# Layer 3 of a four-layer kernel on one core: lanes outside the heads in the skewed returns, a return per half of the heads, rolls built on 128 partitions, halved key and value blocks, and a new instruction plan

## The reference, cut to what matters

```python
Qf = jnp.fft.rfft(Q, axis=2); Kf = jnp.fft.rfft(K, axis=2)     # K, V padded from 154 to 1024 rows
corr = jnp.fft.irfft(Qf * jnp.conj(Kf), n=Lloc, axis=2)
corr_mean = corr.mean(axis=-1)                                  # (batch, head, shift)
w, idx = jax.lax.top_k(corr_mean, top_k)                        # top_k = 6
w = jax.nn.softmax(w, axis=-1)
rolled = jnp.take_along_axis(V[:, :, None, :, :], shifted[..., None], axis=3)
out = jnp.einsum('bhk,bhkld->bhld', w, rolled)
```

## Time and profile before

| | |
|---|---|
| runs | 1690.18, 1690.42, 1696.91 us, median 1690.42 us |
| span of the profiled execution | 1689.5 us, 0.9 us below the median |
| busy | PE 1316.3 us (78%), DVE 1113.8 (66%), ACT 816.4 (48%), POOL 690.3 (41%) |
| mean granted clock of TensorE | 0.865 |

### The profile page before, as it was taken

One profiled execution on the slowest core, in us unless ns is written; L12 is line 12 of the kernel. 1 busy time (PEld: TensorE's weight loads), 2 busy tenths in 40 slices (PEclk: granted clock), 3 DMA queues, 4 the chain that ended last, 5 costly groups with the idle time before them and its releaser, 6 DMA issues.

```text
span 1689.5 us, 18810 instructions
## 1 busy us (share of the span) xinstructions
PE 1316.3 (78%) x5858; PEld 660.2 (39%) x5858; DVE 1113.8 (66%) x2929; ACT 816.4 (48%) x2055; POOL 690.3 (41%) x705
## 2 busy tenths in 40 slices
PE   5789886756788687586576778768979977886998
PEld 2345443332254334333224433433533533532444
DVE  5542417689986867998989898787732451436355
ACT  2345442757657677565674577567426220310110
POOL 2000000388888888828888688875000100000000
PEclk8789997977889797779587689789989988898999
DMA  5000000376556767717656666654010211021000
GB/s 221 22 1 1 10 5 3 81 180 183 151 158 164 197 155 218 185 36 187 173 165 217 175 176 182 166 153 127 7 16 1 82 39 31 1 51 45 1 13 25
DMA packets 59381, 169.07 MB, mean 100 GB/s; under 512 B 15632, under 2 KB 20304, under 8 KB 58640
## 3 DMA queue, kind: packets, MB, share of 16 engines
q0 software_dynamic: 40960, 134.25, 29.6%
q1 hardware_dynamic: 18320, 33.61, 6.2%
HBM read 163.00 MB, written 4.82 MB: 99 GB/s over the span
## 4 chain that ended last, share of the span: by engine, by line
PE 34%; POOL 31%; issue 12%; DVE 12%; DMA 6%; ACT 4%; SPq 1%; POOLq 0%; DVEq 0%; ACTq 0%
POOL bufR L1841 26%; PE psum L1174 6%; POOL half_sum L1855 4%; PE psum L1040 3%; PE psum L1118 2%; DVE bufB L1531 2%; DMA bufR<-in_table,rowid 2%; PE psum L1097 2%; PE psum L844 2%; PE psum L1052 2%; PE psum L975 2%; PE psum L967 1%; PE psum L811 1%; PE psum L896 1%; PE psum L893 1%
## 5 line engine op out<-in xcount | busy, mean ns | idle before, releaser
L1841 POOL DMA_INDIRECT bufR<-in_table,rowid x512 | 549.1, 1072 | 247.2 <-issue 124.5
L1199 ACT ACTIVATE bufR<-bufR 128x256 f32<-128x256 f32 x512 | 205.6, 405 | 79.8 <-DVE bufR L1404 79.4
L1404 DVE TENSOR_TENSOR bufR<-bufR 128x1024 f32<-128x1024 f32 x128 | 163.1, 1275 | 63.7 <-DMA bufR<-in_table,rowid 63.5
L1040 PE MATMUL psum<-xtf,wf 128*128 128x512 f32 x320 | 158.5, 641 | 29.3 <-DVE x_sb L1467 13.3
L844 PE MATMUL psum<-bufB 32*128 32x308 f32 x768 | 99.8, 597 | 102.5 <-DVE bufB L1531 80.2
L1531 DVE TENSOR_REDUCE bufB<-psum 128x8 f32<-128x1232 f32 x96 | 137.8, 1436 | 50.5 <-PE psum L844 50.2
L1868 POOL TENSOR_TENSOR x_sb<-x_sb,wattn 128x256 f32<-128x256 f32 x16 | 11.0, 728 | 295.4 <-DMA wattn<-in_attn 165.0
L1052 PE MATMUL psum<-wf,bufR 128*128 128x256 f32 x320 | 91.1, 437 | 35.7 <-DVE bufR L1679 33.4
L1208 ACT ACTIVATE bufR<-bufR,ew 128x256 f32<-128x256 f32 x128 | 64.1, 503 | 113.0 <-DVE ew L1412 113.0
L1861 POOL TENSOR_TENSOR x_sb<-x_sb,wattn 128x256 f32<-128x256 f32 x32 | 25.4, 823 | 227.9 <-DMA wattn<-in_attn 169.9
L1467 DVE TENSOR_TENSOR x_sb<-x_sb,psum 128x256 f32<-128x256 f32 x128 | 50.1, 415 | 97.9 <-PE psum L975 62.9
(11 more groups left out here) (236 smaller groups left out, 2534.8 us busy)
## 6 DMA issues: line engine op xcount, KB each, us to landing
bufR<-in_table,rowid POOLq DMA_INDIRECT x512, 4.3
wf<-in_ffn SPq DMA_DIRECT2D x2, 2304.0 KB, 15.3
bufR<-in_ffn SPq DMA_DIRECT2D x1, 2696.5 KB, 17.2
wattn<-in_attn SPq DMA_DIRECT2D x4, 641.0 KB, 6.0
wf<-in_rope SPq DMA_DIRECT2D x4, 512.0 KB, 6.2
bufB<-in_ffn SPq DMA_DIRECT2D x1, 2048.0 KB, 8.4
scr_corr<-bufR SPq DMA_DIRECT2D x16, 128.0 KB, 2.4
bufR<-scr_corr SPq DMA_DIRECT2D x4, 512.0 KB
```

What stands on the lines that cost most here:

```text
L1040: ins = mm(bank(6 + r), gu[:, kt, r, :], xtf[:, kt, :], start=kt == 0, stop=kt == KT - 1)
L1199: own.mark(act(row, row, ACT.Identity, accum_out=dots[:, g % 4, j:j + 1]))
L1404: tt(rows, rows, cast(xg[c % 2][:, i, :].unsqueeze(1), [P, GRP, D]), ALU.mult).then_inc(f1_mu, 1)
L1841: eng.indirect_dma_start(ring[:, s * GRP + j, :], None, io["table"], bass.IndirectOffsetOnAxis(ap=rowid[c % 2][:, at + j:at + j + 1], axis ...
```

## The change

1. The skewed returns have the lanes as their first dimension (16 lanes, 8 heads for the correlation; 16 lanes, 4 heads for the rolls). The partition order inside a half becomes (lane, head), so the stores, the value fetch and the masks are rearranged to match. The fetch of the rolls is now four DMAs of 64 partitions instead of two of 128.
2. Each half g has its own return `cr b g`, behind its own stores, and its own semaphores; `o3 b g` waits only for the rolls of its half.
3. The rolls are built on 128 partitions, 8 per head with 128 positions each. `tw b` on DVE makes the weights, `tw b` on PE copies a head's places and weights to its 8 partitions by one matmul, and `tq b` on DVE makes six `tensor_scalar` of 128x128 and one `reduce_sum`. The copy of the sums out of PSUM is gone.
4. A key or value block is 64 columns for a step instead of 128 (half of the old columns were zeros that no matmul read), 128x640 an instruction; all of them lie side by side, so `ks3 1` and `vs3 1` wait for no other reader.
5. The numbers of the planner are new (`vr` counts 14.0 us instead of 1.6, PREFER holds other offsets, by prefixes of an item), so all engines' lists are in another order, in all layers.

```diff
-            a = add("ACT", ("co", b, g), 1.1, p, attn_free, b and ("SP", ("rr", b - 1)))
-            stored = add("SP", ("cw", b, g), 0.4, a, land=2.5)
-        turned = add("SP", ("cr", b), 0.2, (stored, 0.0), values, land=3.5)
+            a = add("ACT", ("co", b, g), 1.1, p, attn_free, b and ("SP", ("rr", b - 1, 1)))
+            stored = add("SP", ("cw", b, g), 3.6, a, land=2.5)
+            turned = add("SP", ("cr", b, g), 0.6, (stored, 0.0), values, land=4.5)
         p = add("PE", ("tp", b), 1.6, turned, a)
-        t = add("DVE", ("tp", b), 4.0, p)
+        t = add("DVE", ("tp", b), 2.8, p)
         a = add("ACT", ("tp", b), 0.3, t)
-        for n in range(TOPC):
-            t = add("DVE", ("tq", b, n), 1.5 if n else 3.2, a, t)
-        stored = add("SP", ("rw", b), 0.2, t, land=2.2)
-        return add("SP", ("rr", b), 0.2, (stored, 0.0), land=4.5)
+        t = add("DVE", ("tw", b), 1.4, a, t)
+        p = add("PE", ("tw", b), 0.3, t)
+        t = add("DVE", ("tq", b), 2.6, p)
+        stored = add("SP", ("rw", b), 0.8, t, land=2.2)
+        return [add("SP", ("rr", b, g), 1.2, (stored, 0.0), land=4.5) for g in range(2)]
 
     def rolled(b, rolls, values):
         for g in range(2):
-            p = add("PE", ("o3", b, g), 8.7, rolls, values)
+            p = add("PE", ("o3", b, g), 8.7, rolls[g], values)
...
-    keys = [add("DVE", ("ks3", b), 3.0, keys0, attn_free if b else ring_free) for b in range(B)]
-    values = [add("DVE", ("vs3", 0), 3.0, values_in)]
+    keys = [add("DVE", ("ks3", b), 1.5, keys0, ring_free) for b in range(B)]
+    values = [add("DVE", ("vs3", b), 1.5, values_in) for b in range(B)]
     rolls = correlate(0, keys[0], queries_in[:2], values[0])
-    values.append(add("DVE", ("vs3", 1), 3.0, values_in, ("PE", ("co", 0, 1))))
...
-        kind = item[:2] if item[0] in BY_LAYER else item[:1]
-        rank[engine, item] += PREFER.get(engine, {}).get(kind, 0.0)
+        offsets = PREFER.get(engine, {})
+        rank[engine, item] += sum(offsets.get(item[:n], 0.0) for n in range(1, len(item) + 1))
...
+        spread = late[0:H, LC["spread"]]
         c1 = [R(1040 * g, 1040) for g in range(2)]
         c2 = [R(2080 + T * g, T) for g in range(2)]
-        cor, rollw, rollt = R(0, T), R(T, T), [R(2 * T, T), R(3 * T, T)]
-        topw, topj, topjf, rsum3, topm = (R(5440 + 8 * z, 8) for z in range(5))
+        hits, rollw = R(0, TOPC * P).rearrange("p (n t) -> p n t", n=TOPC), R(TOPC * P, P)
+        topjf, topw, topj, rsum3, topm = (R(5440 + 8 * z, 8) for z in range(5))
+        topjw, onto = R(5440, 16), R(5480, 16)
         topj = topj.bitcast(U32)
 
         def kst(b, g):
-            at = bufB[:, g * U * P:(g + 1) * U * P] if b else C(g * U * P, U * P)
-            return at.rearrange("p (u n) -> p u n", u=U)
+            return C((2 * b + g) * U * HALF, U * HALF).rearrange("p (u n) -> p u n", u=U)
 
         def vst(b, g):
-            return C((0 if b else 2 * U * P) + g * U * P, U * P).rearrange("p (u n) -> p u n", u=U)
+            return C((4 + 2 * b + g) * U * HALF, U * HALF).rearrange("p (u n) -> p u n", u=U)
 
         def roll(b, g):
             return qx[b][:, g, :]
...
+            def spread_top(b):
+                eng.wait_ge(tp_w, b + 1)
+                mm(psum[:, 2, 0:16], spread, topjw[0:H, :], start=True, stop=True).then_inc(tp_s, 1)
+
             def out3(b, g):
-                eng.wait_ge(tp_rd, 32 * (b + 1))
+                eng.wait_ge(tp_rd[g], 32 * (b + 1))
                 eng.wait_ge(k3_vb, b + 1)
...
             def keys3(b):
                 ring_left(eng)
-                if b:
-                    attention_left(eng)
-                else:
+                if b == 0:
...
-                shape = [P, U, 8, 16]
-                mask = cast(mask8.unsqueeze(1).unsqueeze(3), shape)
+                shape = [P, U, 16, 4]
+                mask = cast(maskk.unsqueeze(1).unsqueeze(1), shape)
                 for g in range(2):
                     src = k3t[:, g, b * SP_:(b + 1) * SP_].rearrange("p (u s) -> p u s", u=U)
-                    ins = tt(kst(b, g).rearrange("p u (h s) -> p u h s", h=8), cast(src.unsqueeze(2), shape), mask, ALU.mult)
+                    ins = tt(kst(b, g).rearrange("p u (s h) -> p u s h", h=4), cast(src.unsqueeze(3), shape), mask, ALU.mult)
                 ins.then_inc(k3_kb, 1)
...
             def values3(b):
                 ring_left(eng)
-                if b:
-                    eng.wait_ge(co_c, 2)
                 eng.wait_ge(k3_rd, 16 * 32)
-                shape = [P, U, 8, 16]
-                mask = cast(mask8.unsqueeze(1).unsqueeze(3), shape)
+                shape = [P, U, 4, 16]
+                mask = cast(maskv.unsqueeze(1).unsqueeze(3), shape)
                 for g in range(2):
-                    ins = tt(vst(b, g).rearrange("p u (h d) -> p u h d", h=8), cast(v3s[:, 2 * b + g].unsqueeze(2), shape), mask, ALU.mult)
+                    ins = tt(vst(b, g).rearrange("p u (h d) -> p u h d", h=4), cast(v3s[:, 2 * b + g].unsqueeze(2), shape), mask, ALU.mult)
                 ins.then_inc(k3_vb, 1)
             def top(b):
                 r = slice(0, H)
                 eng.wait_ge(co_m, b + 1)
-                own.link(eng.tensor_copy(cor[r, :], psum[r, 0:2, :].rearrange("p a n -> p (a n)")))
-                own.link(eng.max(topm[r, :], cor[r, :]))
-                own.mark(eng.max_index(topj[r, :], topm[r, :], cor[r, :]))
+                cor = psum[r, 0:2, :].rearrange("p a n -> p (a n)")
+                own.link(eng.max(topm[r, :], cor))
+                own.mark(eng.max_index(topj[r, :], topm[r, :], cor))
                 tt(topw[r, :], topm[r, :], cast(topm[r, 0:1], [H, 8]), ALU.subtract).then_inc(tp_n, 1)
 
-            def rolls(b, n):
+            def weights3(b):
                 r = slice(0, H)
-                if n == 0:
-                    weights3(b, r)
-                out = rollt[n % 2] if n else rollw
-                own.link(ts(out[r, :], iota[r, :], topjf[r, n:n + 1], topw[r, n:n + 1], ALU.is_equal, ALU.mult))
-                if n:
-                    own.link(tt(rollw[r, :], rollw[r, :], out[r, :], ALU.add))
-                if n == TOPC - 1:
-                    eng.sem_inc(tp_r, 1)
-
-            def weights3(b, r):
                 eng.wait_ge(tp_n, b + 1)
                 own.wait()
                 own.link(eng.tensor_copy(topjf[r, :], topj[r, :]))
...
-                own.link(ts(topw[r, :], topw[r, :], rsum3[r, 1:2], None, ALU.mult))
+                ts(topw[r, :], topw[r, :], rsum3[r, 1:2], None, ALU.mult).then_inc(tp_w, 1)
+
+            def rolls(b):
+                eng.wait_ge(tp_s, b + 1)
+                own.link(eng.tensor_copy(onto, psum[:, 2, 0:16]))
+                for n in range(TOPC):
+                    own.mark(ts(hits[:, n, :], iota, onto[:, n:n + 1], onto[:, 8 + n:9 + n], ALU.is_equal, ALU.mult))
+                own.wait()
+                eng.reduce_sum(rollw, hits.rearrange("p n t -> p t n"), AX.X).then_inc(tp_r, 1)
 
...
                         for h in range(8):
-                            eng.dma_start(v3s[h * 16:(h + 1) * 16, 2 * b + g], src[h]).then_inc(k3_rd, 16)
+                            r, lane = h // 4 * HALF, h % 4
+                            eng.dma_start(v3s[r + lane:r + HALF:4, 2 * b + g], src[h]).then_inc(k3_rd, 16)
...
             def store_corr(b, g):
                 a = 2 * b + g
                 eng.wait_ge(co_s, 2 * b + g + 1)
+                rows = scr1[a].rearrange("(s r h) n -> r s h n", r=2, h=4)
                 for r in range(2):
                     for N in range(2):
-                        eng.dma_start(scr1[a, half(r), N * 512:(N + 1) * 512], c1[g][half(N), r * 512:(r + 1) * 512])\
-                            .then_inc(co_wr, 16)
-                    eng.dma_start(scr1[a, half(r), T:T + 16], c1[g][half(0), r * 512:r * 512 + 16]).then_inc(co_wr, 16)
-
-            def turn_corr(b):
+                        eng.dma_start(rows[r, :, :, N * 512:(N + 1) * 512], c1[g][half(N), r * 512:(r + 1) * 512])\
+                            .then_inc(co_wr[g], 16)
+                    eng.dma_start(rows[r, :, :, T:T + 16], c1[g][half(0), r * 512:r * 512 + 16]).then_inc(co_wr[g], 16)
+
+            def turn_corr(b, g):
                 attention_left(eng)
-                eng.wait_ge(co_wr, 16 * 12 * (b + 1))
-                for g in range(2):
-                    src = bass.AP(scr1.tensor, (2 * b + g) * P * (T + 16), [[16 * (T + 16), 8], [T + 17, 16], [1, T]])
-                    eng.dma_start(c2[g], src).then_inc(co_rd, 16)
+                eng.wait_ge(co_wr[g], 16 * 6 * (b + 1))
+                src = bass.AP(scr1.tensor, (2 * b + g) * P * (T + 16), [[8 * (T + 16) + 1, 16], [T + 16, 8], [1, T]])
+                eng.dma_start(c2[g], src).then_inc(co_rd, 16)
 
             def store_rolls(b):
                 eng.wait_ge(tp_r, b + 1)
                 for z in range(2):
```

(13 more changed lines are left out.)

53 lines of the change are left out of this document (28 added, 25 removed).

## The result

The changed kernel takes 1636.98 us (median of 4 runs, 1635.19 to 1639.68), the kernel before 1693.66 on the same chip (1690.18 to 1699.21): ratio 0.9673, 95% interval 0.9646 to 0.970. The forecast was 1636 us.

What follows compares the result with a forecast made beforehand. No single engine was taken as the bound, but POOL's fetches and PE's layers 2 and 3, with PE waits to close. Terms -11-22.5-20-3+2 = -54.5 us from 1689.5 gave span 1635, time 1636 us; range 1616 to 1660, 8 in 10.

Steps and rivals of the forecast that it cites:

- The bound: Whole kernel: no single engine bounds it; gains must come where POOL's chain of fetches or PE's chain stands still.
- A: Layer 3's value blocks: the addition to x_sb moves ahead of them, shrinking PE's 10.36 us wait; -11 us, bounds -12.5 to -5.
- The 32 DMAs are as long as before: Step at the value blocks: SP's issue of the value fetch stays at 15.12 us, values there 21 us after `V3`.
- B: Layer 3, round 0: PE's idle and cold matmuls at `tp 0` and `o3 0 0` vanish; -22.5 us, bounds -24 to -16.
- C: Layer 3, round 1: PE's waits at `tp 1`, the `u3` and `o3 1` and cold matmuls shrink; -20 us, bounds -23.5 to -12.
- D: Table fetches: DVE's earlier `ix1` for chunk 2 shortens POOL's longest wait, 22.35 us, to near 19; -3 us.
- The rival that ended slower: Table fetches: POOL misses turns waiting for DVE's additions, 4.61 us each, 12 more cancel the gain; 14 give 1700 us; chance 0.04.
- E: First 60 us: keys of layer 0's second batch row now stand ahead of the first head pair; +2 us, bounds 0 to +5.
- Lanes outside: Layer 3's returns: 16 lanes as first dimension bring the DMA share near 1 instead of 0.51; returns land before PE comes.

Runs made afterwards that it cites:

- e7: Changed kernel with the value DMAs writing 16 adjoining partitions instead of every fourth, output not the reference's; `V3` to the end 405.2 us.
- e4: Changed kernel with values stored in another order in DRAM, fetched by 8 DMAs of 64 partitions instead of 32 of 16; 1625.66 us, ratio 0.9646.
- e10: Kernel before with only the planner's new numbers, old operations, on the chip of e9 and e11; 1675.14 us, ratio 0.9894.
- e2: Changed kernel with the rolls built as before, in one piece on 16 partitions; 1658.41 us, ratio 0.9804.
- e11: Changed kernel, unchanged, profiled again on the chip of e9 and e10; 1634.57 us, ratio 0.9667.
- e9: Kernel before, unchanged, profiled on the chip of e10 and e11; first to last fetch 846.5 us.
- e5: Kernel before with only the planner's new numbers, old operations, on another chip than e10; 1692.39 us, ratio 0.9967.
- e6: Changed kernel with the planner's old numbers, all new operations kept; 1666.26 us, ratio 0.9802.
- e8: Version of e4 with the keys of layer 0's second batch row put back behind the first head pair's score work; 1644.47 us, ratio 0.9646.
- e1: Changed kernel with each skewed return cut in two DMAs of eight lanes; 1638.31 us, ratio 0.969.

## Why the prediction was right, by its steps

- **The bound.** No single engine, but PE's waits in layer 3: shown. The rounds gave 49.4 of the 58.3 us, at the same matmuls.
- **A, value blocks: -11 forecast, -4.8 measured** (last fetch to `co 0`; -7.6 in one pair of profiles and -1.9 in the other). From the end of `V3` on it is only -3.1 (105.3 and 105.4 before, 102.5 and 102.1 changed). The step that failed is "The 32 DMAs are as long as before". Issue took 20.6 us instead of 15.1, since every DMA now writes each fourth partition (e7), and started 1.7 us later behind `V3`; the values were there 28.2 us after `V3`'s end instead of 21, and PE waited 3.9 to 6.6 us instead of my 1.5. With an issue of 15.2 us (e7) or 5.4 (e4), `V3` to `co 0` is 95.4 and 93.9 us, -10 and -11.4 against before. The new plan with the old operations reaches 95.2 (e10). So the place and the mechanism were right, the gain is the plan's, and one price was wrong: the new order of lanes takes 7 of the 10 us back.
- **B, round 0: -22.5 forecast, -27.8 measured.** Each step stood as I had put it, counted from `co 0 1`: `tp 0` 13.2 us after its end (forecast 13.5), `tw 0` 23.8 (24.7), `o3 0 0` 38.1 (39.9). The term was mis-sized by 5.3 us, in three parts (means of the two pairs). Slow matmuls gave 8.0 us, and I had counted 5.6, in `tp` and `o3` alone; in the profiles shown above they gave 9.1, most of the rest in the last `y2` (3.44 to 1.97 us) and the logits behind it (3.54 to 1.92). Idle time gave 19.9 us where I had 18.3. And the 1.4 us that I had taken off for `tw 0` and waits inside don't show in these sums.
- **C, round 1: -20 forecast, -21.5 measured.** `o3 1` comes 21.2 us earlier relative to `co 1`. The `u3` waits are gone as a consequence of DVE's shorter rolls; e2 brings them back as one wait of 9.52 us.
- **D, the fetches: -3 forecast, -7.2 measured**, but as the mean of -2.2 and -12.2 in two pairs of profiles. Kernels with the new plan and the new operations took 834 to 846 us on these chips, so neither the size nor the cause is shown. POOL's longest wait didn't fall to 19 us as I had said: it is 22.09 and 22.32 us, before 22.35 and 21.25. Counted from the first fetch of all, chunk 2's first one comes 0.5 us earlier in one pair (436.5 instead of 437.0) and 5.4 in the other (433.5 instead of 438.9 in e11 and e9). POOL's last addition ahead of the wait moves with it, by 0.3 and 6.5 us, and the wait between them stays about as long. What does fall is the waits for additions:

```profile
757.09 1.97 POOL L1841 DMA_INDIRECT bufR<-in_table,rowid  x1 [22.09 <-DVE prob L1644]
...
944.06 0.98 POOL L1841 DMA_INDIRECT bufR<-in_table,rowid  x1 [3.86 <-DVE x_sb L1429]
...
1106.73 1.70 POOL L1841 DMA_INDIRECT bufR<-in_table,rowid  x1 [1.61 <-DVE x_sb L1429]
```

  The rival that ended slower, a dozen more of these, did not come: before, POOL waited 10.7 and 12.1 us for additions ahead of fetches, here 6.1 and 5.7.
- **E, the start: +2 forecast, +3.0 measured**, by the plan (e5, e6, e10), but not by the move that I had named (e8).
- **The chance in it.** The time is right to 1 us while the terms are off by 1 to 6 us in both directions: A gave 6 less, B, C and D together 11 more, and E cost 1 more. I also worked from a before of 1690.4 us, which came out at 1693.7 with one more run. The change itself is -56.7 us by the medians and -58.3 by the profiles, against -54.5. That the total agrees so much better than the parts is luck.
- **Lanes outside.** That the rate doubles was right (0.51 to 0.99), and so was that it is hidden (e1). The four DMAs of the rolls write 64 partitions each, in turn on the lower and the upper half of them. From 1376 to 1378 us the first two were in flight while SP issued the other two, and the traffic was 258 GB/s at a share of 0.99. The Trainium skill, "SBUF — State Buffer", section "Can I just issue two DMAs to hit both halves?", has two such transfers serialize at little more than the rate of one. This trace doesn't agree: 258 GB/s is a third more than the 196 GB/s that I had weighed for one. What one such DMA does alone was not measured.

## What to carry to other kernels

Shortening a serial chain pays until other work covers it, and then stops: of three edits that shorten this one, two can each be taken back for 1 to 2 us, and the third costs 24, so price them together and not one by one. Behind a wait of PE count the slow matmuls too: in round 0 they gave a third to a half of what the idle time gave. When a layout moves to suit one transfer, look at what it does to the issue time of every other DMA that writes it: a step of four partitions cost 5.5 us of issue over 32 DMAs (and 7 us of the stretch), and one better order in DRAM took 15 us off the issue.

## What the runs showed of the hardware that I had not expected

- A DMA of 16 partitions x 160 elements took SP 0.434 us to issue when its partitions follow on each other (e7) and 0.602 us when they lie four apart (changed kernel); one of 64 adjoining partitions with four times the elements 0.644 us (e4). These are the usual values; single ones took up to 1.7 us (e8).
- DVE's MAX8 and FIND_INDEX8 over 16x1024 took 1.22 and 1.21 us from PSUM, and the same from SBUF in the kernel before.
- The stretch of table fetches took 834 to 847 us in every profile but those of e5 to e8, which ran on one chip, and 857 to 861 us there. How much of this is the chip stays open, as said under e5.
- The same matmuls at the same place of the lists ran at different granted clocks in different executions: `V3` took 6.5 us at 1.00 in the changed kernel and 12.0 us at 0.57 in e11, and e5's rounds were 9 us shorter than e10's.
